# Compact 64x64 graph matrices prepared with the attention stream, a values product in four quadrants, and a separate order of steps for each engine, in a four-layer graph kernel

## Chip, cores and metric

One core of one Trainium2 chip. The metric is device time of one execution in microseconds (us), median of the runs.

## What is computed

128 graphs of 64 nodes, 256 features, float32, pass through four layers. `x` is [128,64,256], `adj` is [128,64,64] of zeros and ones, the node mask is all ones in the data but must be honoured.

```python
# layer 0: attention, 8 heads of 64; exp(-adj) and adj are mixed into the probabilities
attn = 0.33*softmax(where(m2, q@k.T/8, -big)) + 0.33*where(m2, adj, 0) + 0.33*exp(-where(m2, adj, big))
x1 = norm(concat_heads(attn @ v) @ W_out + b_out + x)
# layer 1: mean over neighbours
agg = adj @ x1 / max(adj.sum(-1), 1e-6);  x2 = norm(relu([x1, agg] @ W.T) + x1)
# layer 2: hypergraph, with H = (adj != 0), w = first row of adj
Dn = H @ w, inverted where > 0;  Be = H.sum over nodes, inverted where > 0
G = diag(Dn) H diag(Be) H.T
x3 = norm(G @ layernorm(relu(G @ x2 @ W1.T + b1)) @ W2.T + b2 + x2 + x2)
# layer 3: similarity
gate = sigmoid(deg*Wd + bd);  xg = x3*gate;  QK = sigmoid(xg @ Wqk.T + bqk)
S = (QK @ QK.T)*adj, rows divided by their sum
x4 = norm(relu(S @ xg @ Wl.T + bl + xg @ Wr.T) + x3)
```

`norm` is a residual normalisation over the features. The output is x4.

## The kernel before

A group is eight graphs: T = 4 tiles of 128 rows, each tile two graphs (halves h = 0, 1 of the partitions). There are GRP = 16 groups. Dense products run as three products of fp32r high and low parts (`product`, lines 891 to 893): ScalarE copies a PSUM bank out as the high part, VectorE writes the low part (`low_part`, line 605). Everything that has 64x64 matrices is plain float32, and a float32 matmul shows as two instructions in the trace.

Work is a software pipeline. `rounds` (line 295) runs bodies in which four groups are at different stages: stream N (the next group: split of x, projections `q`), stream A (one group behind: attention, layer 0), stream B (one more behind: layers 1 to 3), stream C (last scaling). Fifteen bodies hold both an A and a B; one holds B without A, near the end. One list, `SCHEDULE` (line 42), gives the order of steps, and every engine (TensorE, ScalarE, VectorE, GpSimd) walks through that same list and issues its own share of each step, in order, with semaphores between them. PSUM banks are dealt out by the list: four to A, N and C, four to B (`BANK`), and a step that fills a bank first waits for the reader of the last content (`emptied`).

The graph matrices of a group are made in stream B, between `turn1` (x1 transposed) and `spread`. Per group, SyncE brings `adj` twice: `adjA` [128,4,64] for the attention, and `adjB` [128,4,128], block-diagonal with two graphs to a tile, the zeros written once. Then

- `graph_a`: VectorE makes `edge` = (adjB != 0) in bf16 (line 745), the degree, its inverse; TensorE transposes `edge` (line 1019); ScalarE copies the result twice (lines 533, 534); GpSimd makes `meanA`.
- `graph_b`: TensorE counts with tiny matmuls (lines 1028, 1030); VectorE makes the inverse counts and, in seven small instructions, `dn` (line 771); GpSimd makes `bhT`.
- `graph_m`, `graph_c`, `graph_d`: transpose of meanA (line 1048), product hT0 x bhT (line 1040), transpose of gmat (line 1056), all 128x128.

`agg`, `spread`, `agg3` (`gathered`, line 1067) multiply features by such a block-diagonal matrix, four 128x128 float32 matmuls per feature chunk of 128; `hyper` (line 1109) does it with the matrix stationary; `sim` (line 1125) forms the 128x128 similarity of a tile, of which the diagonal blocks are wanted; `turn_s` (line 1133) transposes it. `score` (line 959) already works with 64x64 operands in all four quadrants of the array, and `pv` (line 984, probabilities times values) with 64x64 operands in the two diagonal quadrants. After the last B-stream norm of a group GpSimd's `split_low` (line 449) makes the low part of the next x.

## Times and profile before

| | |
|---|---|
| median of 3 runs (lowest, highest) | 1361.08 us (1360.6, 1361.57) |
| the profiled execution | 1359.72 us |
| its span on the core | 1357.9 us |
| TensorE matmul busy | 1243.5 us, 92% |
| VectorE / ScalarE / GpSimd busy | 959.6 / 551.9 / 499.2 us |
| mean granted TensorE clock | 0.986 of full |
| DMA | 34.93 MB, 26 GB/s on average |

The rest of a span is time in which an engine stands; a share of busy time says nothing of which wait ends last, so the waits and the order of time have to be read beside it. A matmul's duration holds a tail in which the next already runs: the distance from start to start is what it costs.

### The profile page before, as it was taken

How to read it: one execution, taken by the hardware profiler on the slowest of the kernel's cores; microseconds unless marked ns; L12 is line 12 of the kernel's file. 1: busy time of each engine (PE TensorE's matmuls, PEld its weight loads, DVE VectorE, ACT ScalarE, POOL GpSimd, SP SyncE). 2: the span in 40 equal slices, each digit the busy share in tenths (PEclk: the TensorE clock that was granted, in tenths of full speed). 3: DMA queues.
4: the chain of work that ended last, by engine and by line, in shares of the span. 5: the costliest groups of instructions: out<-in, count | busy, mean ns of one | idle time of the engine just before them, and what ended most of it. 6: DMA issues, size and time to landing. Idle time of an engine off the chain costs nothing.

```text
span 1357.9 us, 30718 instructions
## 1 busy us (share of the span) xinstructions
PE 1243.5 (92%) x11728; PEld 1074.6 (79%) x11728; DVE 959.6 (71%) x2115; ACT 551.9 (41%) x1058; POOL 499.2 (37%) x633
## 2 busy tenths in 40 slices
PE   5699999999999999999999999999999999999776
PEld 4578888788888878887888888878888887888665
DVE  4787676777767677776777777677776767777653
ACT  2344353443534344353444435344353534335221
POOL 2325252442624234261433525244262424425130
PEclk9899999999999999999999999999999999999897
DMA  6000101001010100101010010100101010010000
GB/s 199 21 20 21 36 2 40 15 19 35 11 44 0 39 15 19 35 0 39 15 39 15 19 35 0 39 15 20 34 19 35 0 39 19 0 36 2 20 1 16
DMA packets 43873, 34.93 MB, mean 26 GB/s; under 512 B 19319, under 2 KB 38717, under 8 KB 43838
## 3 DMA queue, kind: packets, MB, share of 16 engines
q1 hardware_dynamic: 43112, 34.04, 8.1%
q10 hardware_dynamic: 726, 0.40, 0.2%
q8 instruction: 24, 0.39, 0.1%
q14 instruction: 11, 0.09, 0.0%
HBM read 26.05 MB, written 8.39 MB: 25 GB/s over the span
## 4 chain that ended last, share of the span: by engine, by line
PE 63%; DVE 22%; issue 9%; ACT 4%; DMA 1%; DVEq 0%; POOL 0%; SPq 0%; ACTq 0%; POOLq 0%
PE bank L891 15%; PE bank L892 14%; PE bank L893 14%; PE bank L1067 5%; DVE x L681 4%; DVE hT_lo L605 3%; PE bank L984 3%; PE bank L959 3%; PE bank L1125 2%; DVE stats L670 2%; PE bank L1011 2%; PE bank L887 2%; DVE smax L713 2%; DVE x L822 2%; DVE yw L833 1%
## 5 line engine op out<-in xcount | busy, mean ns | idle before, releaser
L411 POOL TENSOR_SCALAR var<-mv 128x2 f32<-128x2 f32 (+1 forms) x192 | 42.5, 221 | 683.0 <-DVE mv L674 683.0
L681 DVE TENSOR_SCALAR x<-x,mv,rstd 128x256 f32<-128x256 f32 x256 | 129.7, 553 | 30.0 <-POOL rstd L414 29.9
L503 ACT ACTIVATE hT_hi<-bank 128x512 fp32r<-128x512 f32 x160 | 88.7, 600 | 142.6 <-PE bank L1011 116.2
L414 POOL TENSOR_TENSOR rstd<-var,negh 128x2 f32<-128x2 f32 (+1 forms) x192 | 127.1, 662 | 16.0
L605 DVE TENSOR_TENSOR hT_lo<-bank,hT_hi 128x512 fp32r<-128x512 f32 x160 | 102.9, 683 | 35.0 <-ACT hT_hi L503 30.6
L515 ACT ACTIVATE v<-bank 64x256 f32<-64x256 f32 x256 | 96.8, 378 | 56.5 <-PE bank L893 53.5
L670 DVE BATCH_NORM_STATS2 stats<-x 128x6 f32<-128x256 f32 x256 | 96.4, 419 | 4.4
L520 ACT ACTIVATE prob<-prob 128x512 f32<-128x512 f32 x64 | 40.5, 633 | 127.7 <-DVE prob L715 127.7
L456 POOL TENSOR_TENSOR prob<-prob,srec 128x512 f32<-128x512 f32 x64 | 66.8, 1044 | 65.5 <-DVE srec L723 65.5
L503 ACT ACTIVATE qT<-bank 128x512 f32<-128x512 f32 x64 | 38.3, 598 | 129.0 <-PE bank L893 129.0
L670 DVE BATCH_NORM_STATS2 stats<-r 128x6 f32<-128x512 f32 x64 | 44.5, 695 | 57.2 <-ACT r L503 57.2
L461 POOL TENSOR_TENSOR prob<-prob,mix 128x512 f32<-128x512 f32 x64 | 81.8, 1279 | 6.1 <-POOL prob L456 2.1
L984 PEld LDWEIGHTS bank<-pT,v 64*64 64x64 f32 x2048 | 66.1, 137 | 18.4 <-issue 12.5
L526 ACT ACTIVATE oT_hi<-bank 128x512 fp32r<-128x512 f32 x64 | 38.2, 597 | 102.9 <-PE bank L984 102.9
L984 PE MATMUL bank<-pT,v 64*64 64x64 f32 x2048 | 74.3, 223 | 6.0 <-ACT pT L503 5.9
L891 PE MATMUL bank<-w_hi,hT_hi 128*128 128x256 f32 x256 | 74.1, 290 | 0.2 <-DVE hT_lo L605 0.2
L891 PE MATMUL bank<-wo_hi,oT_hi 128*128 128x256 f32 x256 | 73.2, 286 | 0.5 <-DVE x L730 0.5
L891 PE MATMUL bank<-wm_hi,hT_hi 128*128 128x256 f32 x256 | 72.2, 282 | 0.0
L859 DVE SCALAR_TENSOR_TENSOR x<-bank,x 128x512 f32<-128x512 f32 x32 | 22.1, 692 | 70.0 <-PE bank L893 70.0
L892 PE MATMUL bank<-wo_lo,oT_hi 128*128 128x256 f32 x256 | 71.5, 279 | 0.0
L893 PE MATMUL bank<-wo_hi,oT_lo 128*128 128x256 f32 x256 | 71.4, 279 | 0.0
L892 PE MATMUL bank<-wm_lo,hT_hi 128*128 128x256 f32 x256 | 70.9, 277 | 0.1
(206 smaller groups left out, 3932.9 us busy)
## 6 DMA issues: line engine op xcount, KB each, us to landing
xTin<-in_x_t SPq DMA_DIRECT2D x32, 256.0 KB, 2.9
xin<-in_x SPq DMA_DIRECT2D x16, 512.0 KB, 3.7
out_x<-x SPq DMA_DIRECT2D x32, 256.0 KB, 2.3
adjA<-in_adj SPq DMA_DIRECT2D x16, 128.0 KB, 2.7
adjB<-in_adj SPq DMA_DIRECT2D x32, 64.0 KB, 3.0
r<-in_wqkv SPq DMA_DIRECT2D x2, 512.0 KB, 9.1
x<-in_wqkv SPq DMA_DIRECT2D x1, 512.0 KB, 10.7
x<-in_w_out SPq DMA_DIRECT2D x1, 512.0 KB, 11.0
```

What stands on the lines that cost most here:

```text
L414: pool.tensor_tensor(rstd[layer][:, lo:hi], var[layer][:, lo:hi], negh[:, lo:hi], ALU.pow).then_inc(SEM[f"rstd{n}"], 1)
L461: pool.tensor_tensor(u, u, mix[:, t:t + 2, :].rearrange("p t (a n) -> p t a n", a=1) .broadcast_to([P, 2, HP, N]), ALU.add).then_inc(SEM[" ...
L503: act.activation(dst, src[:, :], func, **kw).then_inc(SEM[ready], 1)
L515: ins = act.activation(v[e * N:(e + 1) * N, i, gr, :, :], src[gr * N:(gr + 1) * N, e], ACT.Copy)
L605: dve.tensor_tensor(lo, src, hi.bitcast(F32), ALU.subtract).then_inc(SEM[f"{name}_lo"], 1)
L670: dve.bn_stats(stats[layer][:, t, :], src[:, t, :]).then_inc(SEM[f"stats{n}"], 1)
L681: ins = dve.tensor_scalar(x[:, t, :], x[:, t, :], mv[layer][:, t, 0:1], rstd[layer][:, t:t + 1], ALU.subtract, ALU.mult)
L891: pe.matmul(out_ap, l[0], rr[0], start=(bias is None and j == 0), stop=False)
L892: pe.matmul(out_ap, l[0], rr[1], start=False, stop=False)
L893: ins = pe.matmul(out_ap, l[1], rr[0], start=False, stop=(j == len(pairs) - 1))
L984: ins = pe.matmul(dst[rows, p * P + gr * N:p * P + (gr + 1) * N], v[rows, i, gr, p, :], pT[rows, i % 2, p, gr * N:(gr + 1) * N], start=Tru ...
L1067: ins = pe.matmul(dst[:, t * P:(t + 1) * P], src[:, t, i * P:(i + 1) * P], mat[:, t, :], start=True, stop=True)
```

## The change

1. Compact matrices. `adjB`, `meanA`, `meanT`, `hT0`, `bhT`, `gmat`, `gT`, the similarity and its transpose are [128,4,64]. Their matmuls take one graph at a time: rows of half h, into partitions of half h (and for `gathered` into a PSUM bank for each half, both feature chunks of a half in one bank). Transposes become matmuls with the identity. Twice as many matmuls, each 64 columns.
2. One round ahead. The steps `graph_a` to `graph_d` belong to stream A now. The matrix hT0 comes from a second, transposed copy of adj by DMA (`adjAt`), so that the transposes of `edge` and the counting matmuls are gone; VectorE counts and sums (`cnt`, `edgew`, `dsum`), with the first row of each adj broadcast by two more DMAs (`wrow`). These DMAs, and the loads of `adjA`, wait for the last readers of the buffers.
3. `pv` runs for two tiles at a time, with odd head pairs written to the other half of the partitions, so that four quadrants are used; the rows of W_out are permuted to match.
4. Each engine has a list of its own (`PE_ORDER`, `ACT_ORDER`, `DVE_ORDER`, `POOL_ORDER`). PSUM banks follow `PE_ORDER`.

In the diff the first `graph_a` and `graph_b` after the DMAs are VectorE's; `pv` and all behind it are TensorE's.

```diff
-SCHEDULE = [
-    ("B", "turn1", 0), ("B", "turn1", 1), ("A", "k", 1), ("B", "graph_a", 0), ("C", "scale3", 0), ("A", "k", 2),
-    ("B", "graph_b", 0), ("B", "graph_m", 0), ("A", "mask", 0), ("A", "k", 3), ("B", "agg", 0), ("B", "agg", 1),
-    ("B", "graph_c", 0), ("A", "mixmat", 0), ("A", "score", 0), ("A", "shift", 0), ("B", "graph_d", 0),
...
+PE_ORDER = [
+    ("A", "k", 1), ("B", "turn1", 0), ("A", "k", 2), ("B", "turn1", 1), ("A", "k", 3), ("B", "agg", 0),
+    ("A", "mixmat", 0), ("B", "agg", 1), ("A", "score", 0), ("B", "mean", 0), ("B", "mean", 1), ("A", "v", 0),
+    ("A", "v", 1), ("A", "v", 2), ("B", "spread", 0), ("A", "score", 1), ("B", "up", 0), ("B", "spread", 1),
+    ("B", "up", 1), ("B", "up", 2), ("B", "up", 3), ("A", "turnp", 0), ("A", "turnp", 1), ("B", "turn_h", 0),
+    ("B", "turn_h", 1), ("B", "turn_h", 2), ("B", "turn_h", 3), ("A", "v", 3), ("A", "pv", 0), ("A", "pv", 1),
+    ("B", "down", 0), ("B", "down", 1), ("B", "hyper", 0), ("B", "hyper", 1), ("A", "graph_c", 0),
+    ("A", "graph_m", 0), ("A", "turnp", 2), ("A", "turnp", 3), ("A", "out0", 0), ("A", "pv", 2), ("A", "pv", 3),
+    ("B", "turn3", 0), ("B", "turn3", 1), ("A", "graph_d", 0), ("N", "q", 0), ("B", "qk", 0), ("B", "qk", 1),
...
+DVE_ORDER = [
...
+    ("B", "up", 0), ("A", "soft", 2), ("B", "up", 1), ("B", "up", 2), ("B", "up", 3), ("B", "turn_h", 0),
+    ("A", "soft", 3), ("B", "turn_h", 1), ("B", "turn_h", 2), ("B", "turn_h", 3), ("A", "graph_a", 0),
+    ("A", "graph_b", 0), ("B", "down", 0), ("A", "pv", 0), ("B", "down", 1), ("B", "hyper", 0), ("A", "graph_c", 0),
+    ("A", "pv", 1), ("B", "hyper", 1), ("B", "gated", 0), ("B", "gated", 1), ("A", "norm0", 0), ("B", "turn3", 0),
...
+POOL_ORDER = [
+    ("B", "mean", 0), ("A", "mask", 0), ("B", "mean", 1), ("A", "soft", 0), ("A", "soft", 1), ("B", "up", 0),
+    ("B", "up", 1), ("B", "up", 2), ("B", "up", 3), ("B", "gate", 0), ("A", "soft", 2), ("A", "graph_a", 0),
+    ("A", "graph_b", 0), ("A", "soft", 3), ("B", "hyper", 0), ("B", "hyper", 1), ("N", "split_low", 0),
...
                     sp.wait_ge(*count("mix_sum", a, 1, 1))
+                    sp.wait_ge(*count("meanA_ready", a, 1, 1))
+                    sp.wait_ge(*count("dsum", a, 1, 1))
                     sp.dma_start(adjA[:, :, :], adj_g[a]).then_inc(SEM["adjA_in"], 16)
+                    for h in range(2):
+                        sp.dma_start(wrow[h * N:(h + 1) * N, :, :], adj_w[a, h, 0:1, :, :]
+                                     .broadcast_to([N, T, N])).then_inc(SEM["wrow_in"], 16)
+                    sp.wait_ge(*count("ht_ready", a, 1, 1))
+                    sp.dma_start(adjAt[:, :, :], adj_tg[a]).then_inc(SEM["adjAt_in"], 16)
...
             def graph_a(g, i):
 
-                dve.wait_ge(*count("adjB_in", g, 32))
-                dve.tensor_scalar(edge[:, :, :], adjB[:, :, :], 0.0, None, ALU.not_equal).then_inc(SEM["edge_ready"], 1)
-                dve.tensor_reduce(deg[:, :], adjB[:, :, :], AX.X, ALU.add).then_inc(SEM["deg_ready"], 1)
+                dve.wait_ge(*count("adjA_in", g, 16))
+                dve.wait_ge(*count("z_ready", g, 1, 1))
+                dve.tensor_reduce(deg[:, :], adjA[:, :, :], AX.X, ALU.add).then_inc(SEM["deg_ready"], 1)
+                dve.wait_ge(*count("adjAt_in", g, 16))
+                dve.tensor_scalar(hT0[:, :, :], adjAt[:, :, :], 0.0, None, ALU.not_equal).then_inc(SEM["ht_ready"], 1)
...
             def graph_b(g, i):
...
+                dve.scalar_tensor_tensor(out=edgew[:, :, :], in0=adjA[:, :, :], scalar=0.0, in1=wrow[:, :, :],
+                                         op0=ALU.not_equal, op1=ALU.mult).then_inc(SEM["edgew"], 1)
...
+                dve.tensor_reduce(dsum[:, :], edgew[:, :, :], AX.X, ALU.add).then_inc(SEM["dsum"], 1)
...
-                dve.tensor_tensor(dn[:, :], drec[:, :], dpos[:, :], ALU.mult).then_inc(SEM["dn_ready"], 1)
+                dve.scalar_tensor_tensor(out=dn[:, :], in0=dsum[:, :], scalar=0.0, in1=drec[:, :],
+                                         op0=ALU.is_gt, op1=ALU.mult).then_inc(SEM["dn_ready"], 1)
...
             def pv(g, i):
-                pe.wait_ge(*count("pT_ready", g, i + 1))
...
+                if i % 2:
+                    return
+                pe.wait_ge(*count("pT_ready", g, i + 2))
+                pe.wait_ge(*count("v_ready", g, i + 2))
...
+                for k in range(2):
+                    for pair in range(HP // 2):
+                        for gr in range(2):
+                            for odd in range(2):
+                                p = 2 * pair + odd
+                                col = (pair * 2 + k) * P + gr * N
+                                for e in range(2):
+                                    rows, to = slice(e * N, (e + 1) * N), (e + odd) % 2
+                                    ins[odd] = pe.matmul(bank_of("oT", i + odd)[to * N:(to + 1) * N, col:col + N],
+                                                         v[rows, i + k, gr, p, :], pT[rows, k, p, gr * N:(gr + 1) * N],
+                                                         start=True, stop=True, skip_group_check=True)
...
+            def flipped(name, g, src):
...
+                for t in range(T):
+                    for h in range(2):
+                        ins = pe.matmul(dst[square(h), t * N:(t + 1) * N], src[square(h), t, :],
+                                        ident[square(h), square(h)], start=True, stop=True, skip_group_check=True)
...
             def graph_c(g, i):
...
-                    ins = pe.matmul(dst[:, t * P:(t + 1) * P], hT0[:, t, :], bhT[:, t, :], start=True, stop=True)
+                    for h in range(2):
+                        ins = pe.matmul(dst[square(h), t * N:(t + 1) * N], hT0[square(h), t, :], bhT[square(h), t, :],
+                                        start=True, stop=True, skip_group_check=True)
...
-            def gathered(name, g, i, src, mat, halves=None):
...
-                    ins = pe.matmul(dst[:, t * P:(t + 1) * P], src[:, t, i * P:(i + 1) * P], mat[:, t, :],
-                                    start=True, stop=True)
+            def gathered(name, g, src, mat, halves=None):
...
+                for c in range(C):
+                    for t in range(T):
...
+                        for h in range(2):
...
+                            ins[h] = pe.matmul(bank_of(name, h)[:, at], src[square(h), t, c * P:(c + 1) * P],
+                                               mat[square(h), t, :], start=True, stop=True, skip_group_check=True)
...
-                          ready=[count("agg_lo", g, c + 1) for c in range(C)])
+                          ready=[count("agg_lo", g, 2)] * C)
...
-                                 [count("spread_lo", g, c + 1) for c in range(C)]), "up", i)
+                                 [count("spread_lo", g, 2)] * C), "up", i)
...
             def hyper(g, i):
...
+                        ins = pe.matmul(dst[square(h), k * D:(k + 1) * D], gT[square(h), 2 * i + k, :],
+                                        yw[square(h), 2 * i + k, :], start=False, stop=(k == 1), skip_group_check=True)
...
             def simi(g, i):
...
-                        tile = qkT[:, c, t * P:(t + 1) * P]
-                        ins = pe.matmul(dst[:, t * P:(t + 1) * P], tile, tile, start=(c == 0), stop=(c == C - 1))
+                        for h in range(2):
+                            one = qkT[:, c, t * P + h * N:t * P + (h + 1) * N]
+                            ins = pe.matmul(dst[square(h), t * N:(t + 1) * N], one, one, start=(c == 0),
+                                            stop=(c == C - 1), skip_group_check=True)
```

Left out of the diff: ScalarE's and VectorE's copies of the new shapes, the new scratch buffers, the other lists in full.

## Rows read from the trace of the kernel before

**Rows 1.** The page: busy time of TensorE, its share, instructions.
```profile
PE 1243.5 (92%) x11728; PEld 1074.6 (79%) x11728; DVE 959.6 (71%) x2115; ACT 551.9 (41%) x1058; POOL 499.2 (37%) x633
```

**Rows 2.** Busy table of one round: window, length, engines in the order of Rows 1, clock.
```profile
602.00:682.40 80.40, 76.21 (x734) 66.07 (x735) 58.29 (x130) 34.29 (x67) 30.92 (x40) 1.00 0.07 23
```

**Rows 3.** mixmat, once a round: in order of time, then the line's first and last start.
```profile
87.66 0.28 PE L909 MATMUL bank<-mj,mi 4*128 4x64 bf16 x4
...
  L909 PE MATMUL bank<-mj,mi x64: 184/186/198, 27.4 to 1212.4; 4*128 4x64 bf16 x64
```

**Rows 4.** TensorE's waits: line, what it waited for, us in total, times, longest.
```profile
PE bank L1019 <- DVE edge L745: 26.0, 16, 2.4
PE bank L1011 <- DVE yw L833: 24.6, 16, 3.7
...
PE bank L909 <- DVE mj L692: 12.6, 14, 0.9
PE bank L984 <- ACT pT L503: 5.9, 14, 3.1
```

**Rows 5.** TensorE in order of time: start, extent, line, shapes, count, wait before.
```profile
610.17 1.15 PE L984 MATMUL bank<-pT,v 64*64 64x64 f32 x32
611.25 0.44 PE L1011 MATMUL bank<-ident,yw 128*128 128x128 f32 x2
...
628.56 1.95 PE L1067 MATMUL bank<-bhT,yw 128*128 128x128 f32 x16
630.26 0.48 PE L891 MATMUL bank<-xT_hi,wk_hi 128*128 128x512 f32 x1
...
641.95 0.40 PE L1019 MATMUL bank<-identb,edge 128*128 128x128 bf16 x4 [1.60 <-DVE edge L745]
...
643.64 0.25 PE L1028 MATMUL bank<-onescol,edge 128*128 128x1 bf16 x4
...
644.25 0.66 PE L1048 MATMUL bank<-ident,meanA 128*128 128x128 f32 x4
644.66 0.48 PE L891 MATMUL bank<-xT_hi,wk_hi 128*128 128x512 f32 x1
...
650.71 1.16 PE L959 MATMUL bank<-kT,qT 64*64 64x64 f32 x64
```

**Rows 6.** Weight loads by shape: line, shapes, count, busy us, mean ns, idle before.
```profile
L984 PEld LDWEIGHTS bank<-pT,v 64*64 64x64 f32 x2048 | 66.1, 137 | 18.4 <-issue 12.5 <-ACT pT L503 3.6
...
L1125 PEld LDWEIGHTS bank<-r 128*128 128x128 f32 x256 | 29.9, 192 | 1.7 <-DVE r L814 1.7
...
L1011 PEld LDWEIGHTS bank<-ident,r 128*128 128x128 f32 x256 | 27.8, 141 | 1.8 <-ACT r L503 0.6
```

**Rows 7.** VectorE, then GpSimd, in order of time, around two slow VectorE instructions.
```profile
608.64 0.41 DVE L681 TENSOR_SCALAR x<-x,mv,rstd 128x256 f32<-128x256 f32 x1
609.70 2.64 DVE L681 TENSOR_SCALAR x<-x,mv,rstd 128x256 f32<-128x256 f32 x2
...
646.66 2.07 DVE L771 TENSOR_TENSOR dn<-drec,dpos 128x4 f32<-128x4 f32 x1
...
609.62 2.57 POOL L449 TENSOR_TENSOR xT_lo<-xTin,xT_hi 128x512 fp32r<-128x512 f32 x2
...
646.36 2.36 POOL L402 TENSOR_TENSOR xin<-xin,bout 128x1024 f32<-128x1024 f32 x1
```

**Rows 8.** Groups of instructions: GpSimd's gate and soft steps, VectorE's low part.
```profile
L441 POOL TENSOR_TENSOR r<-r,bd 128x1024 f32<-128x1024 f32 x16 | 38.3, 2396 | 1.3
...
L461 POOL TENSOR_TENSOR prob<-prob,mix 128x512 f32<-128x512 f32 x64 | 81.8, 1279 | 6.1 <-POOL prob L456 2.1
...
L605 DVE TENSOR_TENSOR hT_lo<-bank,hT_hi 128x512 fp32r<-128x512 f32 x160 | 102.9, 683 | 35.0 <-ACT hT_hi L503 30.6
```

**Rows 9.** TensorE in the last body with a B stream and no A stream.
```profile
1278.19 1.03 PE L1011 MATMUL bank<-ident,x 128*128 128x128 f32 x8
...
1291.51 0.37 PE L891 MATMUL bank<-wm_hi,hT_hi 128*128 128x256 f32 x1
```

More of the change, by code:

```diff
@@ L89 @@
     "mixmat": "mm_ready", "q": "q_ready", "k": "k_ready", "v": "v_ready", "pT": "pT_ready", "oT": "oT_lo",
-    "out0": "sum0_ready", "turn1": "turn1_lo", "agg": "agg_lo", "mean": "sum1_ready", "ht": "ht_ready",
-    "cnt": "dsum", "sym": "g_ready", "meanT": "meanT_ready", "gT": "gT_ready", "spread": "spread_lo",
+    "out0": "sum0_ready", "turn1": "turn1_lo", "agg": "agg_lo", "mean": "sum1_ready", "sym": "g_ready", "meanT": "meanT_ready", "gT": "gT_ready", "spread": "spread_lo",
     "up": "relu_ready", "turn_h": "hT_lo", "down": "down_ready", "hyper": "sum2_ready", "turn3": "turn3_lo",
@@ L178, in graph_layers @@
         oT = split("oT", [P, HP, 2 * P])
-        adjB = sb("adjB", [P, T, P])
-        edge = sb("edge", [P, T, P], BF16)
+        adjB = sb("adjB", [P, T, N])
+        adjAt = sb("adjAt", [P, T, N])
+        wrow = sb("wrow", [P, T, N])
+        edgew = sb("edgew", [P, T, N])
         deg = sb("deg", [P, T])
@@ L211, in graph_layers @@
         xg = yw
-        sim = hT0
+        pair_s, sim, sT = two("sim")
         smat = sim
-        sT = bhT
+        lend = sb("lend", [P, 2 * HID + P])
         simsum = sb("simsum", [P, T])
@@ L304, in rounds, with run @@
             body(None, None, None, GRP - 1)
-        def run(steps, n, a, b, c):
+        def run(order, steps, n, a, b, c):
             group = {"N": n, "A": a, "B": b, "C": c}
-            for stream, name, i in SCHEDULE:
+            for stream, name, i in order:
                 if group[stream] is not None and name in steps:
@@ L472, in _ @@
             }
-            rounds(pool, lambda n, a, b, c: run(steps, n, a, b, c))
+            rounds(pool, lambda n, a, b, c: run(POOL_ORDER, steps, n, a, b, c))
         @block.scalar
@@ L1071, in agg @@
             def agg(g, i):
[L1072 to L1073 removed]
+                if i == 0:
+                    pe.wait_ge(*count("meanT_ready", g, 1))
+                    gathered("agg", g, xl[0], meanT)
             def mean(g, i):
@@ L1129, in turn_s @@
                 pe.wait_ge(*count("s_ready", g, 1))
[L1130 to L1134 removed]
+                flipped("turn_s", g, smat)
             def agg3_(g, i):
[L1137 to L1138 removed]
+                if i == 0:
+                    pe.wait_ge(*count("sT_ready", g, 1))
+                    gathered("agg3", g, xg, sT)
             def out3(g, i):
@@ L1149, in _ @@
                 "turn1": lambda g, i: turned("turn1", g, i, xl[0], "x1_ready", 2),
-                "graph_a": graph_a, "graph_b": graph_b, "graph_m": graph_m, "graph_c": graph_c, "graph_d": graph_d, "agg": agg,
+                "graph_m": graph_m, "graph_c": graph_c, "graph_d": graph_d, "agg": agg,
                 "mean": mean, "spread": spread, "up": up,
@@ L1156, in _ @@
             }
-            rounds(pe, lambda n, a, b, c: run(steps, n, a, b, c))
+            rounds(pe, lambda n, a, b, c: run(PE_ORDER, steps, n, a, b, c))
 def kernel(**inputs):
```

272 lines of the change are left out of this document (121 added, 151 removed), and 28 rows, old and new, of tables (ACT_ORDER, DVE_ORDER, PE_ORDER, POOL_ORDER).

## The prediction

> **What bounds the kernel now.** The page first: TensorE's matmuls fill 92% of the span, VectorE is next at 71% [rows 1]. Busy time alone proves nothing for TensorE, so the second view is the busy table of one round in the middle: 76.21 of 80.40 us, at full clock, while VectorE has 58.29, ScalarE 34.29 and GpSimd 30.92 [rows 2]. So a round has 4.2 us in which TensorE stands, and no other engine is near its limit. The period comes from a step that occurs once a round: 14 periods between 87.66 and 1212.4 make 80.3 us each [rows 3]. There are fifteen bodies with both an A and a B stream, so what a round saves counts fifteen times. Third, TensorE's waits [rows 4]. In sixteen rounds it waited 26.0 us for VectorE's `edge`, 24.6 for the gated rows before `turn3`, 12.6 for the mask rows, 5.9 for `pT`: 1.63, 1.54, 0.79 and 0.37 a round, 4.3 together, which is the idle time of rows 2. The kernel is therefore bound by the order of TensorE's instructions plus these waits. A saved TensorE instruction shortens the round as long as its successor is ready; work taken from another engine shortens it only where it stood ahead of one of these waits.
>
> **TensorE, part by part.** Start-to-start distances in time order are the prices [rows 5].
>
> Removed: the bf16 transposes (641.95, 0.40 with the tail of the last, about 0.20 without it) and the counting matmuls (643.64 to 644.25, 0.61). Together -0.81.
>
> `pv`: 32 instructions in the two diagonal quadrants take 1.08 (610.17 to 611.25). `score`, with the same shape in four quadrants, runs 64 in an extent of 1.16, where pv's 32 have 1.15 [rows 5]. The new pv has score's pattern, so four blocks of 1.08 become two: -2.16. This is the best-founded term, since the row does exactly what the edit does.
>
> `graph_c` is eight instructions of 128 columns at 0.106 (sixteen between 628.56 and 630.26 are 1.70), 0.85. It becomes sixteen of 64 in diagonal quadrants. In proportion to pv's block that is 0.54; I take 0.60, because a block is entered and left once whatever its length. -0.25. `sim` is sixteen such, 1.70, and becomes 32 in two column halves: pv's 1.08, -0.62.
>
> The three transposes (`graph_m`, `graph_d`, `turn_s`) cost 0.41 now (644.25 to 644.66): four instructions. As ordinary float32 matmuls they become sixteen small ones, 0.60: three times +0.19, +0.57. `hyper` streams as many columns, two graphs side by side, but leaves and enters the small shape twice: +0.24.
>
> `gathered` (agg, spread, agg3) is the unknown. Sixteen instructions, 1.70, become 32 of 64 columns with a stationary of 64 rows by 128 columns. No row has that shape. The lower bound is pv's pace: 1.08, -0.62 each. The upper is that the two row halves don't overlap: 32 x 0.106 + 0.12 = 3.5, +1.8 each. Between them: a weight load of 128 float32 columns lasts 192 ns and one of 64 columns 137 [rows 6], so a 128-wide load needs some 55 ns more of its tile, and halving the rows and the moving columns doesn't shorten it. If it paces the tile at the full array's 0.106 and the two halves overlap, as score's do, a gather is 16 x 0.106 + 0.12 = 1.82, +0.12 each. I take this, +0.36 for three; it is nearest in load width. Against it stands that the loads of the transposes, also 128 wide, last 141 [rows 6].
>
> The Trainium skill ("TensorE: Matmul & The Clock Gate", section "LDWEIGHTS (loading the stationary operand)") says that a load's time goes with its columns and that 32 rows of 128 columns take as long as 128 rows; rows 6 agree on the columns, no row shows the rows. The skill's "TensorEngine Tiling (Array Packing)", section "Theoretical Speedup", gives up to two times for one small dimension. By the first the gathers bring nothing, by the second about 0.8 us each.
>
> Sum of TensorE's work: -0.81 - 2.16 - 0.25 - 0.62 + 0.57 + 0.24 + 0.36 = -2.67 a round; with the gathers' two ends -4.9 and +2.4.
>
> **Waits that go.** The 1.63 for `edge` goes with its reader. The 0.79 for the mask rows goes: in the old round VectorE's `dn` stands ahead of them and takes 2.07 us for four elements a row [rows 7]; now the graph steps are elsewhere. The 0.37 for pT goes, because `v` 3 stands before pv. Together -2.78. What is late next, by walking the new lists:
>
> The graph steps of VectorE stand behind the low parts of `turn_h` and before `down` 0, and TensorE reaches `hyper` 0 after v, pv and two downs. GpSimd is then in the gate, whose longer instruction is 2.40, and in `soft` 2, whose longer is 1.28 [rows 8]. Rows 7 show what that does: the two scalings at 609.70 take 2.64 where one alone took 0.41, while GpSimd's xT_lo runs 2.57 from 609.62; and dn ends with GpSimd's 646.36 + 2.36. So VectorE instructions from and to SBUF of this kind (the comparison that makes hT0, `edgew`, `dn`) can each stand until a GpSimd instruction ends. Behind them on VectorE are down 0, the low part of pv and down 1, and TensorE's hyper waits for those. Bounds: 0, and one of the longest, 2.4. I take 1.0, as most of the delay fits under v, pv and the downs.
>
> The wait before `turn3` stays: gated 1 again meets `split_low`, and TensorE has about as much between hyper and turn3 as before. 1.54 to 1.74, +0.2. `turnp` 3 needs a bank that VectorE's low part of pv 1 frees, now behind graph_c: +0.3 (0 to 0.7, one low part, rows 8). Before `up` 0 both halves of spread finish together, so two copies and two low parts of 0.68 [rows 8] follow its last matmul, with one score between: +0.4, and +0.1 at spread. I bound these small ones by 0 and 1.6. New waits: +2.0, bounds 0 and 4.
>
> ScalarE loses two copies a round and halves three, VectorE trades a matrix of 512 columns for four of 256: both have over 20 us a round of cover [rows 2], nothing counted. SyncE's queue: adjA, the two broadcasts and adjAt now wait for VectorE's dsum and GpSimd's meanA of the previous group, with xin and adjB queued behind them. All are released before the A stream's out0, over 30 us before the next body reads them: nothing, and if that cover went, each would be a few us at the start of a body.
>
> **The sum.** A round: -2.67 - 2.78 + 2.0 = -3.45, times fifteen -51.8. The body with B alone: from turn1 to the first mean 1278.19 to 1291.51, 13.3 us, is mostly the graph chain [rows 9]; without it turn1, its low parts and one gather remain, some 6: -7. The first body with A gains two pv blocks and gets the graph steps on its VectorE chain: 0. Together -59. The profiled execution took 1359.7, so 1301; the median lies 1.4 above it, hence 1302.
>
> **Rivals.**
> (1) Gathers at pv's pace. For: loads of transposes at 141 ns. Against: 192 for every other 128-wide float32 load. Three times 0.74 over sixteen groups is 35.5: 1266.
> (2) The new waits don't come: the lists leave enough between. 2.0 x 16 = 32: 1270. With (1) 1235.
> (3) They come at their upper bound, GpSimd's gate and soft blocking VectorE's three graph instructions before down: +32: 1334. For: rows 7; GpSimd is busy without a gap there. Against: only one or two of the three should meet a long instruction.
> (4) Slower: the two row halves of a gather don't overlap, in stream B's path three times a round. 3.5 instead of 1.82 is +5.1 a round, 81 in all: 1383. It decides from 0.091 us an instruction (59 us over 16 x 96 is 0.038 above 0.053). Against: score's four quadrants at 64 in 1.16 us show loads of different rows side by side.
>
> The Trainium skill ("TensorEngine Tiling (Array Packing)", section "Key Properties") says that changing the tiling mode drains TensorE, and the change has fourteen small-shape blocks a round for six. Rows 5 bound it: pv's whole block, entering and leaving included, is 1.08, and my prices are whole blocks.
>
> **Chances.** Forecast with its terms as taken (1285 to 1322) 0.45; (1) 0.20; (2), with or without (1), 0.12; (3) 0.14; (4) 0.09. The range is 1255 to 1345: it holds the forecast, most of (1) and (3) and (2) alone, and leaves out (4), (1) with (2), and worse forms of (3). A measurement of this kernel tells about 0.2% from no change. Faster: 0.45 + 0.20 + 0.12 + most of (3), 0.87; within 0.2%: 0.03; slower: (4) and the end of (3), 0.10.
>
> **What would show it.** In the time order of TensorE: a pv block of 64 with an extent near 1.16; graph_m and turn_s near 0.6; gathers at 1.8 (1.1 for rival 1, 3.5 for rival 4). In the waits: the lines of edge and mask gone, the one before turn3 at 20 to 30 us in total, a new one of TensorE's hyper for VectorE's down near 16 us (over 30 for rival 3). In the order of VectorE: hT0, edgew or dn longer than 1 us beside a GpSimd instruction. The period between mixmats near 76.9. The prediction is wrong if the period is below 75 or above 79, and its reason is wrong if TensorE's busy time in a round doesn't fall by about 2.7.

## The result, and the profile after

The changed kernel takes 1412.54 us (median of four, 1410.68 to 1413.63) against 1360.84 (1360.09 to 1361.57) for the kernel before: a ratio of 1.0379, 95% interval 1.0361 to 1.0397. The forecast was 1302 us and faster. It is slower by 52 us, 110 from the forecast and outside its range.

The page of the changed kernel, its rows for TensorE, the granted clock and the DMA queues:

```profile
PE 1255.3 (89%) x13392; PEld 1052.1 (75%) x13392; DVE 947.7 (67%) x2108; ACT 513.5 (36%) x1026; POOL 489.1 (35%) x631
...
PEclk9799999999999999999999999999999999999986
...
q8 instruction: 135, 2.21, 0.6%
```

q8 is the queue that brings instructions; its numbers are packets, MB, share. Two things stand out beside [rows 1]. TensorE's busy time rose by 12 us although work was taken from it, and its instructions from 11728 to 13392, since each block of small products holds twice as many. And q8 moved 135 packets of 16 KB; in the kernel before that line reads 24.

Two rounds in the middle (columns: window, its length, then busy time and count of TensorE, its weight loads, VectorE, ScalarE, GpSimd, then the granted clock), to be read beside [rows 2]:

```profile
572.00:657.00 85.00, 77.73 (x838) 64.94 (x837) 57.67 (x130) 31.94 (x64) 30.33 (x39) 0.96 0.09 26
657.00:742.30 85.30, 77.75 (x839) 65.08 (x838) 57.74 (x130) 31.95 (x64) 30.36 (x39) 0.96 0.09 26
```

A round has grown from 80.4 to 85.1, its granted clock is 0.96 instead of 1.00, and TensorE stands for 7.4 us of it. Its waits (line, what it waited for, total, times, longest), to be read beside [rows 4]:

```profile
PE bank L930 <- issue: 30.5, 12, 2.8
PE bank L1150 <- DVE yw L845: 26.5, 15, 1.8
PE bank L1059 <- DVE yw L871: 23.1, 16, 3.5
PE bank L929 <- issue: 19.4, 12, 2.0
```

The waits for edge and for the mask rows are gone, as forecast. The one for `yw` before turn3 (L1059) stayed. The one before `hyper` (L1150) is the new wait that the forecast put at 16 us; it is 26.5. The remaining two are of no kind that the forecast had: "issue" is time in which the engine waited for nothing that the profile shows. Both come twelve times, once for each return of the loop. TensorE in order of time at one of them:

```profile
660.98 0.49 PE L929 MATMUL bank<-xT_hi,wk_hi 128*128 128x512 f32 x1 [1.76 <-issue]
663.94 0.41 PE L930 MATMUL bank<-xT_lo,wk_hi 128*128 128x512 f32 x1 [2.47 <-issue]
664.17 0.61 PE L931 MATMUL bank<-xT_hi,wk_lo 128*128 128x512 f32 x1
664.57 0.63 PE L929 MATMUL bank<-xT_hi,wk_hi 128*128 128x512 f32 x1
...
667.82 0.39 PE L929 MATMUL bank<-xT_hi,wk_hi 128*128 128x512 f32 x1
```

One product of 512 columns, a stop of 1.76 us before it and one of 2.47 behind it; then the same products are 0.42 us apart, and 0.23 only from 667.8 on. The second half of the price is the clock, in steps of 2 us:

```profile
662.00:664.00 2.00, 0.06 (x1) 0.06 (x1) 0.00 (x0) 0.00 (x0) 0.27 (x1) 1.00 0.00 0
664.00:666.00 2.00, 2.00 (x6) 1.48 (x6) 0.00 (x0) 0.00 (x0) 0.00 (x0) 0.55 0.00 0
666.00:668.00 2.00, 2.00 (x9) 1.76 (x8) 0.42 (x1) 1.45 (x3) 0.00 (x0) 0.60 0.04 8
668.00:670.00 2.00, 2.00 (x12) 1.63 (x12) 2.00 (x6) 1.09 (x2) 0.00 (x0) 1.00 0.00 0
```

After a stretch in which TensorE did next to nothing, the clock is granted at 1.2 instead of 2.4 GHz for some 3.4 us, from 664.2 on; at half speed that is 1.7 us of lost work, an estimate. A stretch of this kind follows the stops in each of the twelve rounds (6.8 us long in three of them), and a second one follows the wait before hyper in eleven. Together they are 7.4 us a round at half clock, which is why TensorE's busy time rose: it falls to 1228.8 us in the first experiment below.

The suspicion behind the experiments comes from two counts. Between two of its branch records TensorE leaves 1529 records of instructions in the kernel before and 1732 in the changed one (the expectations count the compiled program, where it is one or two more). Of the 135 packets of q8, 108 fall into the twelve rounds, nine in each; before, none did. So the suspicion is that TensorE's loop no longer stays in its instruction memory from one return to the next; below, a loop that stays is called resident, one that is brought again is refetched.

### The profile page after: what moved, and what is told of

It reads as the page before. It is cut to its first block, busy times and chain, and to the rows that moved or that the text cites. A ratio compares the mean times of both kernels' runs of the same rounds, so it can differ in the third digit from the quotient of the medians.

```text
span 1408.9 us, 33937 instructions
## 1 busy us (share of the span) xinstructions
PE 1255.3 (89%) x13392; PEld 1052.1 (75%) x13392; DVE 947.7 (67%) x2108; ACT 513.5 (36%) x1026; POOL 489.1 (35%) x631
## 3 DMA queue, kind: packets, MB, share of 16 engines
q8 instruction: 135, 2.21, 0.6%
## 4 chain that ended last, share of the span: by engine, by line
PE 69%; DVE 21%; issue 8%; ACT 2%; DMA 1%; POOL 0%; SPq 0%; DVEq 0%; POOLq 0%
PE bank L929 17%; PE bank L930 15%; PE bank L931 15%; PE bank L1107 7%; PE bank L1155 3%; PE bank L1059 3%; DVE hT_lo L637 3%; DVE x L717 2%; DVE hyperedge L784 2%; DVE spT_lo L643 1%; DVE yw L871 1%; PE bank L925 1%; PE bank L1072 1%; PE bank L998 1%; PE bank L1174 1%
## 5 line engine op out<-in xcount | busy, mean ns | idle before, releaser
L717 DVE TENSOR_SCALAR x<-x,mv,rstd 128x256 f32<-128x256 f32 x256 | 116.9, 506 | 2.4 <-POOL rstd L441 2.3
L528 ACT ACTIVATE kT<-bank 128x512 f32<-128x512 f32 x64 | 38.2, 598 | 201.8 <-PE bank L931 201.8
L528 ACT ACTIVATE pT<-bank 128x512 f32<-128x512 f32 x64 | 38.3, 598 | 126.4 <-PE bank L1009 126.2
L930 PE MATMUL bank<-xT_lo,wk_hi 128*128 128x512 f32 x128 | 56.6, 443 | 30.5 <-issue 30.5
L929 PE MATMUL bank<-xT_hi,wk_hi 128*128 128x512 f32 x128 | 61.9, 483 | 19.4 <-issue 19.4
L929 PE MATMUL bank<-wo_hi,oT_hi 128*128 128x256 f32 x256 | 74.1, 289 | 3.3 <-DVE oT_lo L637 3.3
L929 PE MATMUL bank<-wm_hi,hT_hi 128*128 128x256 f32 x256 | 74.5, 291 | 1.3 <-DVE hT_lo L637 1.0
L929 PE MATMUL bank<-w_hi,hT_hi 128*128 128x256 f32 x256 | 74.0, 289 | 0.2 <-DVE hT_lo L637 0.2
L931 PE MATMUL bank<-wm_hi,hT_lo 128*128 128x256 f32 x256 | 72.8, 284 | 0.0
L931 PE MATMUL bank<-wo_hi,oT_lo 128*128 128x256 f32 x256 | 72.4, 283 | 0.0
L930 PE MATMUL bank<-w_lo,hT_hi 128*128 128x256 f32 x256 | 72.0, 281 | 0.0
```

The source lines that it names most:

```text
L528: act.activation(dst, src[:, :], func, **kw).then_inc(SEM[ready], 1)
L717: ins = dve.tensor_scalar(x[:, t, :], x[:, t, :], mv[layer][:, t, 0:1], rstd[layer][:, t:t + 1], ALU.subtract, ALU.mult)
L929: pe.matmul(out_ap, l[0], rr[0], start=(bias is None and j == 0), stop=False)
L930: pe.matmul(out_ap, l[0], rr[1], start=False, stop=False)
L931: ins = pe.matmul(out_ap, l[1], rr[0], start=False, stop=(j == len(pairs) - 1))
```

## The experiments

The kernel before ran beside each of them; its median was 1360.3 to 1360.8 us. Ratios are against it. A pair of idle lines moves source lines by two: L929 of the changed kernel is L931 in those with the increments.

### Is it the instruction fetch?

**Loop moved by 64 idle instructions**

```diff
         def _(pe):
+            for _ in range(64):
+                pe.sem_inc(parted, 1)
             pe.wait_ge(setup_dve, 1)
```

> The changed kernel with 64 idle semaphore increments put at the very start of TensorE's program, where it waits for weights anyway; the loop body stays the same, only its position in the program moves. Theory F (instruction fetch): TensorE stands 4.2 us at every return of its loop with nothing in the profile to wait for, because its loop (1733 instructions, 1530 before) no longer stays in its instruction memory; how many 16 KB blocks the loop touches depends on where it starts, so one of the three shifts (64, 128, 192 of a block's 256) should let it fit: then 12 returns times (4.2 us and some 2 us of half clock behind each) go, about 1338 us, and the instruction queue falls from 135 packets to some 35; a shift that doesn't fit stays at 1412. Theory W (the waits of the new orders and the gathers' price made it slow): 1412 for every shift. Theory B (the branch back itself costs, whatever is resident): 1412 for every shift.

1334.65 us in one run. Moving the loop by 64 instructions and nothing else took 78 us off, where theories W and B both had 1412. q8:

```profile
q8 instruction: 27, 0.44, 0.1%
```

No wait for issue at the loop's return is left, and the waits before hyper and turn3 are what they were (26.6 and 23.1).

**By 128 and by 192** (the same edit with other counts)

> The same with 128. Theory F: either about 1338 us with some 35 instruction packets, or 1412 with 135; at least one of the three shifts gives the former. Theories W and B: 1412.

> The same with 192. Theory F: either about 1338 us with some 35 instruction packets, or 1412 with 135; at least one of the three shifts gives the former. Theories W and B: 1412.

1361.29 and 1375.15 us (one run each), 135 packets each: refetched, but at neither of the two times that theory F allowed. The stop at the return is one of 1.6 us instead of two:

```profile
PE bank L931 <- issue: 19.7, 12, 1.9
```

In the second of them the line reads 51.0 in 13 times with a longest of 30.4: that one comes once, ahead of the loop, and the other twelve make 20.6. So whether the loop is refetched depends on where it starts, and what the refetching costs does too: the same nine packets a round, 4.2 or 1.6 us of standing. By the fit further below, only 4 to 11 of the changed kernel's loop records lie in the loop's first block, and 132 to 139 and 68 to 75 with the moves by 128 and 192. In all three a packet starts 0.9 to 1.6 us behind the branch and the next one at 4.0 to 4.7. That the second stop is the wait for that next packet, which the longer first blocks cover, fits these times and isn't tested by itself.

**No loop at all**

```diff
-            with eng.Fori(1, GRP - 2) as g:
+            for g in range(1, GRP - 2):
```

> The changed kernel with the loop of the compute engines written out (13 bodies in a row instead of one body 13 times), so that no engine but SyncE branches back. Theory F: fetching ahead in a straight line is hidden, as it is in the bodies before the loop, so about 1338 us. Theory B: about 1338 too. Theory W: 1412. F and B are told apart by the shifts.

1335.41 us (four runs; ratio 0.9809, 0.9785 to 0.9832). All instructions are new and are brought (107 packets), but in line, with no branch back, and no wait for issue at a round's start is left. Fetching in line costs nothing that this run shows (1335.4 beside 1334.7 resident); coming back to a place that is no longer there does.

**The kernel before, made longer**

```diff
-                now_full(product(dst[:, :], [(chunk(w, c, slice(i * P, (i + 1) * P)), chunk(xT, c)) for c in range(C)]), name, i)
+                for half in range(2):
+                    cols = slice(half * 256, (half + 1) * 256)
+                    ins = product(dst[:, cols], [(chunk(w, c, slice(i * P, (i + 1) * P)), chunk(xT, c, cols)) for c in range(C)])
+                now_full(ins, name, i)
```

> The kernel before, with each 512-column product of q and k split into two of 256 columns: 48 more matmuls and loads in TensorE's loop (1627 instructions instead of 1530), the same columns streamed. Its loop touches 7 blocks of 256 instructions. Theory F (TensorE stands where its loop no longer fits its instruction memory; the border lies between 7 and 8 blocks): no instruction fetches inside the loop, no wait put down to issue at its return, 1361 to 1375 us (split products cost at most 0.02 us each, 0 to 1 us a round). Rival C (more instructions cost time one by one wherever they lie, and that is what the changed kernel lost): 96 of the 203 added instructions, so about half of what they cost, 1395 to 1410.

> The same kernel with 64 idle semaphore increments ahead of TensorE's first instruction, so that the same loop of 1627 instructions lies across 8 blocks of 256. Theory F: about 9 instruction fetches a round, waits for issue of 1.7 to 4.2 us at each return of the loop, 20 to 75 us over the unshifted one. Rival C, and a rival by which the refetching is a matter of the changed kernel alone (its orders, its small shapes): same time as the unshifted one within 3 us.

The answer came with the labels exchanged. The unshifted one, which was to be resident, took 1372.0 us (ratio 1.0079, 1.0059 to 1.0099) with 133 packets:

```profile
q8 instruction: 133, 2.18, 0.7%
```

and these waits of TensorE:

```profile
PE bank L1014 <- issue: 19.7, 12, 1.9
...
PE bank L1022 <- DVE edge L745: 12.1, 15, 2.4
```

The shifted one, which was to be refetched, took 1362.77 (ratio 1.0014, 1.0004 to 1.0025) with 25:

```profile
q8 instruction: 25, 0.41, 0.1%
```

no wait for issue at the loop's return, and

```profile
PE bank L1024 <- DVE edge L745: 25.7, 16, 2.4
```

Rival C is out: 96 more instructions a round cost nothing where the loop stays resident (+2 us in all). The mechanism isn't a matter of the changed kernel: it came back in the old one. The border was wrong, though. And the price was 9 us, not 20: of a stop of 1.64 a round a part falls into the wait for edge, which shrank from 25.7 to 12.1 in all. A stop ahead of a wait on other engines is partly free; in the changed kernel no wait follows as soon.

**The border, once more.** Six cases fit one rule if the blocks of 256 begin 44 to 48 instructions ahead of the compiled program's first one and a loop stays where it touches seven of them at most. A move by 16 tells this from a count without the offset.

> The changed kernel with 16 idle semaphore increments ahead of TensorE's first instruction. So far the loop of 1733 instructions was fetched again at a start moved by 0, 128 and 192 and not at 64; one of 1627 was fetched again as it stood and not when moved by 64. Counted from the compiled program's first instruction, these six cases don't fit one border. They fit if a loop stays resident where it touches at most 7 blocks of 256 and the blocks begin 44 to 48 instructions earlier than that count. By this (theory F with the offset) a move of 16 is resident: no fetches in the loop, 1330 to 1340 us. By the rival, blocks counted without an offset and the other cases by something else, 16 is across 8 blocks: 108 fetches in the loop, 1355 to 1412 us.

1331.66 us (ratio 0.979, 0.9771 to 0.981), 27 packets. The rule with the offset foretold this case; a count from zero would have had it refetched. What the 44 to 48 instructions are, and whether the rule holds for loops of other lengths, stays open: it is a fit, with one case foretold.

The fit can be redone on the traces. Counted in TensorE's records, loads and matmuls included, the loop of the changed kernel begins at record 2715, that of the kernel before at 2410 and that of the longer old one at 2662. With blocks that begin 90 to 97 records ahead of the first record, all thirteen kernels here that have a loop come out right, refetched where it touches eight blocks and resident at seven or fewer; limits of five, six or eight blocks fit them at no offset. The offset is another than the 44 to 48 above, which is in instructions of the compiled program; the traces don't hold that count. Of the thirteen, only the move by 16 was foretold.

The Trainium skill ("Runtime: NRT & Kernel Launch", section "Instruction fetch mechanics") gives TensorE an instruction memory of 2048 instructions, refilled in blocks of 256, 16 KB each, ahead of use and in order, and says that a taken branch to a page outside the current window of two stalls the engine. The packets agree with the block (2.21 MB by 135 is 16 KB), and so does the stop behind the branch. The window of two doesn't: loops of 1529 to 1732 instructions, which span six blocks and more, came back without a packet. Seven resident blocks and one being fetched would make that 2048, an estimate that no run here tests by itself.

### What of the rest?

With the loop resident the kernel takes about 1334 us, 32 above the forecast. Two of its rounds, with a wait before hyper in each:

```profile
551.00:628.50 77.50, 74.16 (x838) 62.98 (x837) 57.64 (x130) 31.93 (x64) 30.40 (x39) 1.00 0.09 27
628.50:707.50 79.00, 75.69 (x838) 63.88 (x838) 57.67 (x130) 31.93 (x64) 30.38 (x39) 0.98 0.09 27
```

Both are of the kernel moved by 64. The second has a stretch at half clock; eight of twelve rounds have one. It begins at 674.0, just behind the wait before hyper:

```profile
672.80 0.39 PE L1152 MATMUL bank<-bias,ones 96*128 96x256 bf16 x2 [1.75 <-DVE yw L845]
673.12 1.13 PE L1157 MATMUL bank<-yw,gmat 64*64 64x256 f32 x8
...
674.72 1.97 PE L1157 MATMUL bank<-yw,gmat 64*64 64x256 f32 x8
```

The same eight products take 1.13, then 1.97. So the new wait costs its own 1.75 us (1.78 in most rounds), and 1.5 more in two rounds of three (79.0 against 77.5 us). What it waits for is VectorE's chain of graph steps ahead of `down` 0. VectorE, then GpSimd, of the changed kernel in order of time:

```profile
614.96 1.74 DVE L784 TENSOR_SCALAR hyperedge<-adjAt 128x256 f32<-128x256 f32 x1
616.62 1.00 DVE L786 TENSOR_SCALAR degm<-deg 128x4 f32<-128x4 f32 x1
...
617.98 1.00 DVE L795 TENSOR_SCALAR cntm<-cnt 128x4 f32<-128x4 f32 x1
618.90 0.41 DVE L797 SCALAR_TENSOR_TENSOR edgew<-adjA,wrow 128x256 f32<-128x256 f32 x1
...
619.80 0.58 DVE L804 TENSOR_SCALAR dsafe<-dsum 128x4 f32<-128x4 f32 x1
...
620.63 0.75 DVE L808 SCALAR_TENSOR_TENSOR dn<-dsum,drec 128x4 f32<-128x4 f32 x1
```

```profile
614.16 2.38 POOL L466 TENSOR_TENSOR r<-r,bd 128x1024 f32<-128x1024 f32 x1
616.51 1.09 POOL L481 TENSOR_TENSOR prob<-prob,srec 128x512 f32<-128x512 f32 x1
617.68 1.28 POOL L486 TENSOR_TENSOR prob<-prob,mix 128x512 f32<-128x512 f32 x1
618.92 0.87 POOL L448 TENSOR_TENSOR mean<-adjA,rdeg 128x256 f32<-128x256 f32 x1
619.75 0.61 POOL L455 TENSOR_TENSOR hyperedge<-hyperedge,be 128x256 f32<-128x256 f32 x1
620.32 1.04 POOL L481 TENSOR_TENSOR prob<-prob,srec 128x512 f32<-128x512 f32 x1
```

hT0 (`hyperedge` in the trace) ends at 616.70, degm at 617.62, cntm at 618.98, dsafe at 620.38 and dn at 621.38; GpSimd's instructions end at 616.54, 617.60, 618.96, 620.36 and 621.36. Each of these five ends with a GpSimd one, whatever its size: four elements a row cost up to a microsecond. The reductions and reciprocals between them don't (on average 406 to 420 ns and 162 to 178 ns).

**The graph steps elsewhere.** The comparison, the counts, edgew and dn go behind `soft` 2, where GpSimd is idle; the degree stays, since the gate still reads the old one.

```diff
+    ("B", "up", 0), ("A", "soft", 2), ("A", "graph_b", 0), ("B", "up", 1), ("B", "up", 2), ("B", "up", 3), ("B", "turn_h", 0),
...
-    ("A", "graph_b", 0), ("B", "down", 0), ("A", "pv", 0), ("B", "down", 1), ("B", "hyper", 0), ("A", "graph_c", 0),
+    ("B", "down", 0), ("A", "pv", 0), ("B", "down", 1), ("B", "hyper", 0), ("A", "graph_c", 0),
```

(hT0 and cnt move from VectorE's `graph_a` into its `graph_b`.)

> The changed kernel with the 64 idle increments of the resident case (its base, 1334.7 us), and the graph steps of VectorE that need no degree (comparison of the transposed adjacency, counts, weighted edges, dn) moved from behind turn_h to behind soft 2. Theory H (what is left over of the miss is the wait before hyper, 1.77 us a round, and the half clock that follows it, 3.4 us at half speed in 12 of the rounds, 1.7 each): the wait falls below 0.5, the half-clock stretch at graph_c goes, period 78.5 to 75.5, 1285 to 1298 us. Rival G (the rest of the miss lies in the gathers, 1.95 for 1.82, and other blocks, the wait only moves on to turn3 or the banks): 1320 to 1335.

1290.6 us (1288.13 to 1293.56, ratio 0.9488, 0.9469 to 0.9507), as theory H had it. The groups of VectorE in this kernel (last number: mean ns):

```profile
L791 DVE TENSOR_SCALAR hyperedge<-adjAt 128x256 f32<-128x256 f32 x16 | 3.9, 244 | 0.0
...
L795 DVE TENSOR_SCALAR cntm<-cnt 128x4 f32<-128x4 f32 x16 | 3.1, 191 | 0.5
...
L784 DVE TENSOR_SCALAR degm<-deg 128x4 f32<-128x4 f32 x16 | 28.8, 1799 | 0.6
```

On average hT0 fell from 1645 to 244 ns and cntm from 994 to 191 by their place alone; degm, left behind, fell in with the gate's second instruction and rose from 954 to 1799. The wait before hyper is gone, and with it every stretch at half clock inside the loop; all rounds have this length:

```profile
532.00:607.50 75.50, 73.84 (x838) 62.93 (x837) 55.57 (x130) 31.92 (x64) 30.11 (x39) 1.00 0.09 28
```

The Trainium skill ("SBUF — State Buffer", section "SBUF: two separate sides") describes this as one pair of ports between VectorE and GpSimd, which the first to start locks for its whole instruction, against VectorE operations in a two-port mode or with two SBUF inputs. This trace, which doesn't show the mode of an operation, agrees in both directions: hT0, degm, cntm, dsafe and dn stood, the reductions didn't, and `edgew`, which started at 618.90, took its 0.41 while GpSimd's next, at 618.92, took 0.87 where it takes 0.61 in the moved kernel.

**Without the shift**

> The changed kernel with the moved graph steps alone, TensorE's program where it stood (no idle increments). If the two costs, refetching and the wait before hyper with its half clock, are separate and add: 1290.6 + 75 = 1365 us (1350 to 1372), the fetches and the waits for issue as in the changed kernel. If the wait before hyper had been a consequence of the refetching, or hides part of it: under 1340.

1367.68 us (ratio 1.0055, 1.0035 to 1.0075), with 135 packets and 46.8 us of waits for issue, within the 1350 to 1372 of the first case. The two costs are separate: refetching is worth 78 us with the wait before hyper (1412.5 to 1334.7) and 77 without it (1367.7 to 1290.6). The better order by itself would still have lost to the kernel before.

**The values product alone, on the kernel before.** Only `pv`, its copies, and the rows of W_out.

```diff
-                pe.wait_ge(*count("pT_ready", g, i + 1))
+                if i % 2:
+                    return
+                pe.wait_ge(*count("pT_ready", g, i + 2))
...
-                            ins = pe.matmul(dst[rows, p * P + gr * N:p * P + (gr + 1) * N], v[rows, i, gr, p, :],
+                                    rows, to = slice(e * N, (e + 1) * N), (e + odd) % 2
+                                    ins[odd] = pe.matmul(bank_of("oT", i + odd)[to * N:(to + 1) * N, col:col + N],
```

> The kernel before with the values product alone in four quadrants (pv, its copies and the order of the rows of the output weights; nothing else). The prediction's term: four blocks of 1.08 us become two, 2.16 us a round, so 1361 - 33 = 1328 (1322 to 1335), TensorE's wait for edge and for yw before turn3 unchanged. Rival S (what TensorE saves ahead of a wait comes back as a longer wait): the wait before turn3 grows from 24.6 us by up to 20, 1340 to 1350. A first pv that waits for two pT instead of one can add up to 0.6 a round in either.

1363.66 us (1362.60 to 1366.68, ratio 1.0026, 1.0016 to 1.0036): no gain at all from the best-founded term, and neither expectation held. Its waits, to be read beside [rows 4]:

```profile
PE bank L1018 <- DVE yw L831: 29.8, 16, 3.7
PE bank L1026 <- DVE edge L743: 26.1, 16, 2.4
PE bank L990 <- ACT pT L503: 15.3, 15, 3.6
```

and two of its rounds:

```profile
474.60:554.40 79.80, 74.29 (x734) 64.15 (x734) 58.13 (x130) 34.13 (x66) 30.98 (x39) 1.00 0.07 23
554.40:635.80 81.40, 75.87 (x735) 65.49 (x734) 58.35 (x130) 34.24 (x66) 31.16 (x39) 0.98 0.07 23
```

TensorE's busy time fell by 1.9 us (76.21 to 74.29, full clock), close to the term's 2.16. Waits took 1.3 of it back: 0.6 for pT, since the first block now needs two transposed tiles, 0.4 for `yw` (1.44 to 1.82 us in a round of the loop), the rest in small ones. And eight rounds of twelve pay 1.6 more for half clock behind that wait; the kernel before has no such stretch inside its loop. That the longer wait, with less work around it, brings the half clock is argued from where the stretch stands, not shown by itself.

**The same term the other way**, in the kernel with the moved steps: pv back in two quadrants (48 idle increments, so that the loop stays resident).

> The moved graph steps (base 1290.6 us, resident), with the values product back in two diagonal quadrants, four blocks of 32 a round instead of two of 64; nothing else undone. Theory P (the prediction's term of 2.16 us a round holds where the waits about pv are covered; in the kernel before it gave 0.6 only, since pT, oT_lo and yw came late and half clock followed): period 75.5 to 77.6, 1321 to 1327 us. Rival S (TensorE's saved time there is mostly waited away here too): under 1308.

1306.52 us (1304.21 to 1307.44, ratio 0.9602, 0.9586 to 0.9618), 16 more than with four quadrants. That is under rival S's 1308, just; of theory P's 2.16 a round the period shows 1.0 (75.5 to 76.5 us). TensorE in order of time, this kernel (a view that ends at 670, which cuts its last row short), then the one with four quadrants:

```profile
666.54 2.08 PE L1027 MATMUL bank<-pT,v 64*64 64x64 f32 x64
668.55 0.44 PE L1054 MATMUL bank<-ident,yw 128*128 128x128 f32 x2
669.41 0.76 PE L1054 MATMUL bank<-ident,yw 128*128 128x128 f32 x5 [0.42 <-DVE yw L873]
```

```profile
657.68 1.16 PE L1033 MATMUL bank<-pT,v 64*64 64x64 f32 x64
658.78 0.44 PE L1061 MATMUL bank<-ident,yw 128*128 128x128 f32 x2
660.56 0.87 PE L1061 MATMUL bank<-ident,yw 128*128 128x128 f32 x6 [1.34 <-DVE yw L871]
```

2.01 against 1.10 from start to start: going over to four quadrants saves 0.91 at each of the two places of pv, and behind the second one 0.92 stands as a longer wait before turn3. The first place pays, the second doesn't: 1.0 a round, 16 us.

**The wait before turn3.** The second scaling of VectorE takes 2.65 us there, beside both halves of GpSimd's `split_low`. They go apart:

```diff
-    ("A", "graph_b", 0), ("A", "soft", 3), ("B", "hyper", 0), ("B", "hyper", 1), ("N", "split_low", 0),
+    ("A", "graph_b", 0), ("A", "soft", 3), ("B", "hyper", 0), ("N", "split_low", 0), ("B", "hyper", 1), ("N", "split_low", 1),
...
-                for c in range(C):
+                for c in [i]:
```

> The moved graph steps (base 1290.6 us, resident), and GpSimd's two halves of split_low apart: one in its idle stretch between the two square roots of hyper, one where both stood. The second scaling of VectorE ahead of turn3, 2.65 us beside GpSimd's 2.57, should take 1.3; TensorE's wait before turn3 falls from 1.34 us a round to below 0.3, period 75.5 to 74.3, 1270 to 1276 us. Rival: the wait is for the chain hyper, mean and variance, square root, scaling itself, and the first half delays the second square root: 1285 to 1295.

1280.02 us (1279.47 to 1280.99, ratio 0.9412, 0.9397 to 0.9428). The scaling takes 1.70, and the wait

```profile
PE bank L1061 <- DVE yw L871: 10.4, 16, 3.5
```

is 10.4 us in all, 23.6 with both halves together: 0.39 to 0.48 in a round of the loop, down from 1.34 to 1.43 but not under 0.3, and the period is 74.6. The time lies between the two expectations, nearer to the first. Of the versions here this is the fastest, 80 us below the kernel before.

## Why the prediction was wrong

**The step that failed** is the price of an instruction. "A saved TensorE instruction shortens the round as long as its successor is ready" counts time from start to start, and the doubled counts (gathers, sim, flips, graph_c, hyper) were priced by the blocks' durations alone. Taken together those prices held (below). What had no term was the sum of the counts: 203 more instructions in the loop, which then, where it stood, didn't stay in the instruction memory. None of the rivals was this mechanism; the slower one was about the gathers, and it is false. So the period was 85.1 where the forecast had 76.9 and called itself wrong above 79, and TensorE's busy time in a round rose where it was to fall by 2.7. Refetching cost 78 us of the 110.5: 4.2 us a return for the two stops and 2.4 for half clock, 6.6 by twelve. Most of the 2.4 stands behind the stops; part of it is that the wait before hyper is followed by half clock in eleven rounds of twelve here, in eight of the resident kernel. Nothing in the rows of before prices it, but its profile had the line to ask about: 24 instruction packets, of which the trace has none within the loop. With the kernel's text, from which the number of instructions in a round can be counted, the question could have been put.

**The new wait at hyper** was seen, with its place and its cause, and put too low: 1.0 a round, "as most of the delay fits under v, pv and the downs", and since "only one or two of the three should meet a long instruction". There were not three such instructions but five (hT0, degm, cntm, dsafe, dn), and all five met one, because GpSimd has almost no gap there and one that has stood starts the next just in time to stand again; `edgew`, one of the three that the prediction named, didn't stand. The wait was 1.77, and the half clock behind it, 1.5 in two of three rounds, wasn't in the sum at all. Moving the steps gave 44 us where the forecast had 16: 28 more of the miss. The mechanism is the one that the forecast itself and rival 3 gave; the wait of 26.5 us lies between their 16 and over 30. That the resident kernel's 1334.7 meets rival 3's 1334 is chance: rival 3 had new waits of 4.0 a round and no half clock.

**The rest** is 4.6 us: with both out, 1290.6 stands against the 1302 - 16 = 1286 that the sum gives without the wait at hyper. Period 75.5 against 75.9; TensorE's busy time in a round -2.4 (76.21 to 73.84) against -2.67. So the miss that is left isn't in the loop, whose twelve periods gained 5.6 us more than foretold: of the 21.6 us that the forecast gives the work ahead of them and behind them, the profiled executions show 12.5. Which instructions there fell short stays open. Term by term, in that kernel or the changed one:
- pv: a block of 64 in 1.16, as foretold, and two blocks save 1.8 to 2.1 of the 2.16. But of the block in front of the wait before turn3 nothing arrives: putting pv back cost 1.0 a round, and pv alone on the kernel before gave nothing. The sum has the full 2.16 here; that its total came out right all the same is luck, owed to the other new waits (spread, up, turnp: 0.8 foretold), of which this trace has 0.2 in a round.
- Gathers: the row is plain,

```profile
670.45 2.00 PE L1107 MATMUL bank<-mean,x 64*128 64x64 f32 x32
```

 2.0 against 1.95 in [rows 5], 1.93 to 1.96 from start to start against 1.70 to 1.78. So +0.65 for the three and not +0.36: the halves overlap (rival 4 is false), but nothing is won (rival 1 is false). The weight loads of 64 rows by 128 columns last 188 to 198 ns with the moved steps; those of the gathers in the kernel before, 128 rows by 128 columns, last 192 to 209. Of the two rules of the Trainium skill that the prediction weighed, the one of "TensorE: Matmul & The Clock Gate", section "LDWEIGHTS (loading the stationary operand)", agrees with these loads; the gain that "TensorEngine Tiling (Array Packing)", section "Theoretical Speedup", allows came in pv and sim, whose stationary is 64 columns wide, and not in the gathers, whose stationary is 128.
- From start to start, at full clock: graph_m 0.56, graph_d and turn_s 0.61, graph_c 0.46 (0.60 foretold for each), sim 1.08, hyper +0.10 against +0.24: right or a little better. These small gains make up for the gathers.
- edge and mask waits gone, turn3 at 23.1 in total (20 to 30 foretold): right.

So the sum was within half a microsecond a round for what it counted, in part because errors cancelled, and the kernel was slower for what it didn't count.

## What to carry to other kernels

Where a change adds instructions to a loop, count them for each engine, and look at the instruction queue of the page: packets inside the loop mean that it is being brought again at every return, and 16 idle instructions ahead of it were worth 5.7% of the time here (1412.5 to 1331.7 us). Where VectorE's comparisons, maxima and products between SBUF tiles stand beside a busy GpSimd, count each of them, however small, as ending with a GpSimd instruction (five of six did here; reductions and reciprocals didn't), and put them where GpSimd is idle. Price TensorE's time up to the next wait, not by itself: a saving just ahead of a wait comes back as a wait, and the wait can cost the clock as well.

## What was not expected of the hardware

A loop of 1732 instructions on TensorE runs with or without fetches by where it starts: refetched with its start moved by 0, 128 and 192, resident with 16 and 64; one of 1625 is refetched as compiled and resident when moved by 64. The same nine packets a round stop TensorE for 4.2 us at one start and for 1.6 at others. A wait of some 1.8 us was followed by 3.4 us at half clock in eight of twelve rounds (the kernel moved by 64, and pv alone on the kernel before) and in eleven of twelve in the changed kernel; ones of 1.34 to 1.60 (before turn3, at edge) in none. That is no border: the single stops at a return, 1.4 to 2.0 us, were followed by half clock in two rounds of twelve with the moves by 128 and 192 and in one of the longer old kernel.
